# Third attention layer: raw keys stored by token class, loaded without copies in two buffers, spread by a broadcast

## The chip, the cores and the metric

The kernel runs on one core of a Trainium2 chip. The metric is the device time of one execution in microseconds (us); the median of several runs is compared. Engines: PE (TensorE) multiplies matrices, DVE (VectorE), ACT (ScalarE) and POOL (GpSimd) work on tiles of 128 partitions in the on-chip memory, SP (SyncE) issues the DMAs here. SPq and its like in the rows are the queues of an engine, in which DMAs are issued. Each engine executes its own instructions in order and waits on semaphores.

## The reference, cut to what matters

Four pairs of an attention and a feed-forward layer on 2048 tokens of width 128, each with layer norms and a residual. The change lies in the attention layer of the third pair, which sees 4 batches of 512 tokens with 16 heads of width 8:

```python
qkv = (x @ w_qkv.T).reshape(B, N, 3, H, hd).transpose(2, 0, 3, 1, 4)
q, k, v = (qkv[0] * scale, qkv[1], qkv[2])
attn = jnp.einsum('bhid,bhjd->bhij', q, k)
idx = _rp_bucket(N)[None, None]              # clip(j - i, -31, 31) + 31
qL = jnp.einsum('bhid,hdm->bhim', q, rpe_k_table)
attn = attn + jnp.take_along_axis(qL, idx, axis=-1)
kL = jnp.einsum('bhjd,hdm->bhjm', k * scale, rpe_q_table)
attn = attn + jnp.swapaxes(jnp.take_along_axis(kL, idx, axis=-1), 2, 3)
attn = jax.nn.softmax(attn, axis=-1)
out = jnp.einsum('bhij,bhjd->bhid', attn, v)   # + a term of rpe_v_table
```

The term kL belongs to a key j and depends on the distance to the query i. Near the diagonal (distance up to 31) it differs from entry to entry; these are the key bands.

## The kernel before, in words

`l2_attn` is one stage of the program, with a prep block and a main block. P is 128 partitions, T * P is 2048 tokens, B is 4, N is 512, HD is 8, GRP is 32, HALF is 16.

The prep block makes queries, keys and values for all heads, one pass per batch. ACT evacuates PE's products (`L2262` to `L2265`); the fourth of these, `L2265`, writes the scaled keys in float32 into a buffer of two slots, `base[:, b % 2, 2, :]`. PE multiplies it with `gw` (`L2297`), and SP stores it to the DRAM tensor `k32` (`L2157`), 128 rows of 512 tokens. It is the first of ten stores of a batch; the others (`L2160`, `L2164`) write bfloat16 parts of queries and keys. Two semaphores, `stored`, count them by slot; from the third batch on ACT waits for all stores of the batch before last. After them come the stores of `g` and `rv`. The block ends when all engines and stores are done.

The main block runs over 16 heads of 8 steps each, every engine through its own loop over the steps. In a step PE computes the scores of two blocks of 32 queries in all batches (`scores`), DVE adds the band (`L2526`), takes the maximum (`L2528`) and later transposes the probabilities (`L2535`) that ACT has made with exp (`L2609`). Between these PE has other work in its fixed order: in the steps 1 to 3 of head h the key bands of head h+1 (`key_bands`, `L2652`, three rounds), in steps 4 to 7 the query bands of head h+3, and the products with the values.

For the key bands each token's key must stand alone on its partitions. There are 16 classes of tokens, the token number modulo 16. Tile `xk` has on partition 8 i + d component d of the keys, with all tokens zero but those of class 15 - i. It is made per head by three things: SP's `keys(h)` loads `rawk`, in which each of the 8 rows of the head stands 16 times (a source dimension with step 0; 8 KB per partition), and behind it `kshift`, both waited on by semaphores; `expand(h)` on POOL multiplies `rawk` with the mask `own_shift` into `xk` (`L2465`); PE waits for it before the first round. There is one `rawk` and one `xk`. `expand(h + 2)` stands in POOL's order in step 7 of head h, behind `combine(h + 1)` (`L2473`, `L2475`: waits for the load of the query bands `qb` and for the key bands `kb`), `values(h + 1)` (`L2451`, `L2455`) and `cut` (`L2480`: waits for the load of `sb`, the probabilities near the diagonal). `keys(h + 2)` stands in SP's order in step 4 of head h, behind the loads of `qs` and `ks` for head h+1 (`L2350` to `L2354`) and the stores and loads of `pband` (`L2394` to `L2407`). The sources of `qb` and `sb` are skewed: 4 batches, then 32 rows, then the elements.

Of the kernel before, what the change touches and what calls it, by code (L numbers as in the profile page):

```python
# [7 lines left out]
F32 = mybir.dt.float32  # L8
# [6 lines left out]
B = 4  # L15
# [2037 lines left out]
def l2_scratch(nc):  # L2053
    return {"q3": nc.dram_tensor("l2_q3", (P, len(Q_PARTS), T * P), BF16).ap(),
            "k3": nc.dram_tensor("l2_k3", (P, len(K_PARTS), 2, T * P), BF16).ap(),
            "g3": nc.dram_tensor("l2_g3", (2, HEADS, 3, T * P), BF16).ap(),
            "k32": nc.dram_tensor("l2_k32", (P, T * P), F32).ap(),
            "rel": nc.dram_tensor("l2_rel", (P, KEY_SHIFTS), F32).ap(),
            "rv": nc.dram_tensor("l2_rv", (HEADS, P, BAND), F32).ap(),
            "qband": nc.dram_tensor("l2_qband", (QBAND_RING, P, ROW + GRP), F32).ap(),  # L2060
            "pband": nc.dram_tensor("l2_pband", (PBAND_RING, P, HROW + GRP), F32).ap()}


def l2_attn(nc, xs, c, w, scratch):
# [4 lines left out]
    with ExitStack() as ctx:  # L2069
# [18 lines left out]
                 "ones_ready once_ready hl0 hl1 kl kt0 kt1 rl0 rl1 l_ps l_ready qw0 qw1 qw2 qr0 qr1 pw0 pw1 pw2 sr0 sr1 tabq_ready "  # L2088
# [4 lines left out]
        head_loaded = [m["hl0"], m["hl1"]]  # L2093
        shifts_loaded = [m["kt0"], m["kt1"]]
# [16 lines left out]
        with ExitStack() as prep, nc.Block() as block:  # L2111
# [19 lines left out]
            def _(sp):  # L2131
# [22 lines left out]
                for b in range(B):  # L2154
                    cols = slice(b * N, (b + 1) * N)
                    sp.wait_ge(m["base_ready"], 4 * b + 4)
                    sp.dma_start(k32[:, cols], base[:, b % 2, 2, :]).then_inc(stored[b % 2], 16)  # L2157
# [89 lines left out]
            def _(a):  # L2247
# [7 lines left out]
                for b in range(B):  # L2255
# [9 lines left out]
                    a.activation(base[:, b % 2, 2, :], ps_q[1], ACT.Copy, scale=SCALE).then_inc(m["base_ready"], 1)  # L2265
# [10 lines left out]
            def _(pe):  # L2276
# [14 lines left out]
                for b in range(B):  # L2291
# [5 lines left out]
                    pe.matmul(ps_g[2 * HEADS * b:2 * HEADS * (b + 1), :], gw[:, :, :].rearrange("p a h -> p (a h)"), base[:, b % 2, 2, :], start=True, stop=True).then_inc(m["gam_ps"], 1)  # L2297
# [13 lines left out]
        rawk = s.sb("rawk", [P, T * P])  # L2311
# [19 lines left out]
        with nc.Block() as block:  # L2331
            @block.sync
            def _(sp):
                def keys(h):

                    if h:
                        sp.wait_ge(m["xk_ready"], h)
                    src = bass.AP(k32.tensor, k32.offset + h * HD * T * P, [[0, HALF], [T * P, HD], [1, T * P]])
                    sp.dma_start(rawk[:, :], src).then_inc(m["kl"], 16)
# [100 lines left out]
            def _(g):  # L2440
# [19 lines left out]
                def expand(h):  # L2460

                    g.wait_ge(m["kl"], 16 * (h + 1))
                    if h:
                        g.wait_ge(m["l_ps"], ROUND["k", h - 1, KEY_ROUNDS - 1])
                    g.tensor_tensor(xk[:, GRP:GRP + T * P].rearrange("p (g c) -> p g c", c=HALF), rawk[:, :].rearrange("p (g c) -> p g c", c=HALF),  # L2465
# [949 lines left out]
```

## Time and profile before

| | |
|---|---|
| median of 3 runs | 2537.59 us (2532.54 to 2545.24) |
| the profiled execution's own time | 2533.08 us |
| its span, first to last instruction | 2531.3 us |
| mean granted TensorE clock | 0.859 |
| busy: PE, DVE, ACT, POOL | 1916.8, 1696.1, 1089.0, 851.6 us |
| `L2465`, the expansion, 16 times | 72.2 us busy, 73.9 us of waiting for `rawk` before |
| loads of `rawk` | 16 of 1024 KB, 13.3 us from issue to landing in the median |

In all rows times are microseconds from the start of the span. "[3.85 <-POOL l2a_xk L2465]" means that the engine had been idle for 3.85 us, ended by what POOL's line 2465 wrote. PE's records may be slightly off, as matmuls are pipelined. The stage of the change is found in the span from about 1464 to 2050 us.

### The profile page before, as it was taken

Reading aid. Unit: us, or ns where it says so; the run is one execution under the profiler, and the core shown is the slowest. Engines: PE = TensorE matmul, PEld = TensorE weight load, DVE = VectorE, ACT = ScalarE, POOL = GpSimd, SP = SyncE. Lnnn points to the kernel's source line nnn. Section 1 sums busy time; section 2 is a strip of 40 time slices with the busy share of each in tenths; the row PEclk is TensorE's granted clock in tenths of the full one; section 3 lists DMA queues with packets and bytes.
Section 4 is the critical chain, followed back from the end, with each engine's and each line's share of the span. In section 5 each row is a group of like instructions: output and inputs, shape, how many; then the busy total and the mean of one; then the engine's idle time right before and its main releaser. Section 6 shows DMA issues by size and latency. Waiting matters only on the chain. (4 is left out here: it accounts for less than half of the span.)

```text
span 2531.3 us, 46421 instructions
## 1 busy us (share of the span) xinstructions
PE 1916.8 (76%) x16420; PEld 1318.0 (52%) x16420; DVE 1696.1 (67%) x4018; ACT 1089.0 (43%) x2022; POOL 851.6 (34%) x630
## 2 busy tenths in 40 slices
PE   5888886587778876449999846878878747999666
PEld 2555554255555553337777614444444336888444
DVE  4777777676555564668999951788887857223574
ACT  2666664354445542204444421555555412333442
POOL 3000000774455430113344333445454319900211
PEclk8999999799999898659999965698888757999678
DMA  3011110200000000010000046566665432000000
GB/s 104 30 39 40 40 38 2 80 16 16 16 16 16 16 16 1 5 22 11 21 21 16 5 133 172 145 175 174 169 178 166 119 122 89 26 8 1 6 1 19
DMA packets 126969, 144.92 MB, mean 57 GB/s; under 512 B 73222, under 2 KB 100673, under 8 KB 123992
## 3 DMA queue, kind: packets, MB, share of 16 engines
q1 hardware_dynamic: 123542, 132.82, 18.9%
q10 hardware_dynamic: 3266, 9.96, 1.0%
q8 instruction: 99, 1.62, 0.3%
q14 instruction: 62, 0.51, 0.1%
HBM read 94.46 MB, written 40.81 MB: 53 GB/s over the span
## 5 line engine op out<-in xcount | busy, mean ns | idle before, releaser
L454 ACT ACTIVATE l0a_pr<-l0a_sm,l0a_nm 128x512 f32<-128x512 f32 x256 | 185.1, 724 | 142.6 <-DVE l0a_nm L367 142.1
L367 DVE CUSTOM_DVE_ANT_0 l0a_sm<-l0a_ps_s,l0a_tb 128x512 f32<-128x512 f32 x256 | 170.8, 685 | 87.6 <-PE l0a_ps_s L522 84.7
L2609 ACT ACTIVATE l2a_pr<-l2a_ps_s,l2a_nm 128x512 f32<-128x512 f32 x256 | 173.8, 685 | 116.6 <-DVE l2a_nm L2528 115.6
L530 PE MATMUL l0a_ps_p<-top_c_ident,l0a_pr 128*128 128x128 f32 x1024 | 168.9, 288 | 54.4 <-ACT l0a_pT L462 54.2
L530 PEld LDWEIGHTS l0a_ps_p<-top_c_ident,l0a_pr 128*128 128x128 f32 x1024 | 109.3, 142 | 116.5 <-ACT l0a_pr L454 65.1
L2528 DVE TENSOR_REDUCE l2a_nm<-l2a_ps_s 128x2 f32<-128x1024 f32 x128 | 156.7, 1224 | 4.4
L2535 DVE STREAM_TRANSPOSE l2a_tt<-l2a_pr 128x1024 f32<-128x1024 f32 x128 | 158.0, 1234 | 0.1
L1557 POOL TENSOR_TENSOR l1f_h<-l1f_lm,l1f_sg 128x512 f32<-128x512 f32 x72 | 92.5, 1285 | 184.9 <-DVE l1f_lm L1626 184.9
L807 POOL TENSOR_TENSOR l0f_ct<-l0f_raw,l0f_cos_scaled 128x1024 f32<-128x1024 f32 x32 | 76.7, 2397 | 174.0 <-issue 94.2
L1929 ACT ACTIVATE l2f_h<-l2f_ps_h 128x512 f32<-128x512 f32 x128 | 76.5, 598 | 135.8 <-PE l2f_ps_h L1474 129.8
L1684 ACT ACTIVATE l1f_csb<-l1f_ps_c,l1f_b3e 128x512 f32<-128x512 f32 x128 | 88.1, 688 | 106.0 <-PE l1f_ps_c L1474 105.7
L2705 PE MATMUL l2a_ps_o<-l2a_tt,l2a_vd 128*32 128x256 f32 (+7 forms) x1472 | 124.3, 376 | 0.0
L1042 PE MATMUL l0f_ps_side<-l0f_wqkv,l0f_hT 128*128 128x512 f32 x192 | 110.5, 667 | 15.9 <-ACT l0f_hT L953 9.5
L2526 DVE TENSOR_TENSOR l2a_ps_s<-l2a_ps_s,l2a_qb 128x192 f32<-128x192 f32 (+2 forms) x160 | 45.7, 304 | 113.2 <-PE l2a_ps_s L2676 69.0
L1887 DVE SCALAR_TENSOR_TENSOR l2f_acc<-l2f_ps_y,l2f_comb,l2f_acc 128x128 f32<-128x128 f32 x112 | 31.5, 344 | 134.0 <-PE l2f_ps_y L1967 134.0
L1967 PEld LDWEIGHTS l2f_ps_y<-l2f_w2T,l2f_h 128*128 128x128 f32 x1024 | 119.1, 192 | 2.8
L1967 PE MATMUL l2f_ps_y<-l2f_w2T,l2f_h 128*128 128x128 f32 x1024 | 119.3, 275 | 0.0
L336 POOL COPY l0a_vh<-l0a_va 128x128 f32 x14 | 4.1, 293 | 326.6 <-PE l0a_ps_o L541 326.6
L2652 PE MATMUL l2a_ps_l<-l2a_xk,l2a_kshift 128*32 128x256 f32 x768 | 74.0, 519 | 50.5 <-POOL l2a_xk L2465 48.2
L522 PE MATMUL l0a_ps_s<-l0a_ks,l0a_qs 48*128 48x512 bf16 x256 | 100.9, 395 | 8.1 <-issue 7.6
L823 POOL TENSOR_TENSOR l0f_rn<-l0f_ss,top_c_half 128x16 f32<-128x16 f32 x32 | 95.0, 2970 | 33.5 <-DVE l0f_ss L904 32.5
L2465 POOL TENSOR_TENSOR l2a_xk<-l2a_rawk,l2a_masks 128x2048 f32<-128x2048 f32 x16 | 72.2, 4515 | 73.9 <-DMA l2a_rawk<-l_k 73.9
(522 smaller groups left out, 5190.5 us busy)
## 6 DMA issues: line engine op xcount, KB each, us to landing
l2a_rawk<-l_k SPq DMA_DIRECT2D x16, 1024.0 KB, 13.3
l2a_qb<-l_qband SPq DMA_DIRECT2D x16, 768.0 KB
l2a_sb<-l_pband SPq DMA_DIRECT2D x32, 384.0 KB
l_qband<-l2a_staged SPq DMA_DIRECT2D x14, 768.0 KB, 15.1
l0a_tb<-l_bias SPq DMA_DIRECT2D x16, 448.0 KB
l2a_ks<-l_k SPq DMA_DIRECT2D x16, 384.0 KB
l_pband<-l2a_pr SPq DMA_DIRECT2D x32, 192.0 KB, 8.7
l_pband<-l2a_pr SPq DMA_DIRECT2D x32, 144.0 KB, 2.2
```

The lines of the kernel that those rows point to most:

```text
L367: v.tensor_tensor_reduce(sm[j % 4][:, :], ps_s[j % 2][:, :], tb[slot][:, off:off + N][:, ::-1], -1.0, 3e38, ALU.add, ALU.min, nm[:, j % 4: ...
L454: a.activation(pr[j % 4][:, :], sm[j % 4][:, :], ACT.Exp, bias=nm[:, j % 4:j % 4 + 1], scale=-1.0).then_inc(m["p_ready"], 1)
L522: pe.matmul(ps_s[j % 2][:, :], qs[slot][:, b * N + it * P:b * N + (it + 1) * P], ks[slot][:, b * N:(b + 1) * N], start=True, stop=True).th ...
L530: last = pe.transpose(ps_p[j % 2][:, tile(k)], pr[j % 4][:, tile(k)], ident[:, :])
L823: g.tensor_tensor(rn[:, u, :], ss[:, u, :], c["half"][:, :], ALU.pow).then_inc(m["rn_ready"], 1)
L1042: last = pe.matmul(bank[:, :], hT[:, tile(t)], wqkv[:, l, i * F_INNER:(i + 1) * F_INNER], start=True, stop=True)
L1557: g.tensor_tensor(h[b % 2][:, k, :], lm[:, k, :], sg[:, k, :], ALU.mult).then_inc(h_ready, 1)
L1967: last = pe.matmul(ps_y[b % 2][:, t, :], h[b % 2][:, k, t * P:(t + 1) * P], w2T[slot][:, k, :], start=(k == 0), stop=(k == FC - 1))
L2528: v.tensor_reduce(nm[:, g % 2, :], ps_s[g % 2][:, :, :], AX, ALU.max, negate=True).then_inc(m["nm_ready"], 1)
L2535: v.transpose(tt[n % 2][:, u * NB:(u + 2) * NB, :].rearrange("p (u k) i -> p u (k i)", u=2), pr[g // 2 % PR_RING][:, 2 * (g % 2):2 * (g % ...
L2609: a.activation(pr[slot][:, 2 * (g % 2) + u, :], ps_s[g % 2][:, u, :], ACT.Exp, bias=nm[:, g % 2, u:u + 1], accum_out=rs[:, n % 2, 2 * (g % ...
L2705: last = pe.matmul(ps_o[n % 2][GRP * g:GRP * (g + 1), (lo - a0) * GRP:(hi - a0) * GRP], vd[h % 2][:, v, k, :], tt[n % 2][:, block:block + ...
```

## The change

The raw keys are stored, loaded and read in another layout.

- Store: `L2265` writes the keys of a batch sorted by class, class 15 first, and SP stores them to `k32`, now (128, 16 classes, 4 batches, 32 tokens): runs of 32 elements, 128 bytes. PE's product with `gw` reads the sorted keys through a view that gives the tokens in their old order and writes to the same places.
- Load: partition 8 i + d gets only the tokens of class 15 - i, 128 elements, 512 bytes, without copies. There are two `rawk` buffers with a semaphore each, and the wait ahead of the load is for the expansion two heads earlier.
- Expansion: POOL's first operand is the loaded 128 elements, each read 16 times in a row by a broadcast; mask, output and count of elements stay.

```diff
--- before.py
+++ after.py
@@ -2054,7 +2054,7 @@
     return {"q3": nc.dram_tensor("l2_q3", (P, len(Q_PARTS), T * P), BF16).ap(),
             "k3": nc.dram_tensor("l2_k3", (P, len(K_PARTS), 2, T * P), BF16).ap(),
             "g3": nc.dram_tensor("l2_g3", (2, HEADS, 3, T * P), BF16).ap(),
-            "k32": nc.dram_tensor("l2_k32", (P, T * P), F32).ap(),
+            "k32": nc.dram_tensor("l2_k32", (P, HALF, B, N // HALF), F32).ap(),
             "rel": nc.dram_tensor("l2_rel", (P, KEY_SHIFTS), F32).ap(),
             "rv": nc.dram_tensor("l2_rv", (HEADS, P, BAND), F32).ap(),
             "qband": nc.dram_tensor("l2_qband", (QBAND_RING, P, ROW + GRP), F32).ap(),
@@ -2085,12 +2085,13 @@
         ps_l = s.ps("ps_l", [P, N])
         names = ("w_loaded t_loaded m_loaded rv_loaded zero_ready zeroed wt_ready wT_ready zb_ready t_ready zT_ready qk_ps base_ready hi_ready res_ready "
                  "mid_ready lo_ready q_lo gam_ps gam_ready g_lo g_stored v_ps va_ready tab_ready tab_stored rvd_ready rvd_stored st0 st1 "
-                 "ones_ready once_ready hl0 hl1 kl kt0 kt1 rl0 rl1 l_ps l_ready qw0 qw1 qw2 qr0 qr1 pw0 pw1 pw2 sr0 sr1 tabq_ready "
+                 "ones_ready once_ready hl0 hl1 kl0 kl1 kt0 kt1 rl0 rl1 l_ps l_ready qw0 qw1 qw2 qr0 qr1 pw0 pw1 pw2 sr0 sr1 tabq_ready "
                  "s_ps biased nm_ready p_ready tT xk_ready added comb_ready sm_ready vs_ready masked st_ready vd_ready pv_done o_ps oe_ready u_ps rr_ready o_done "
                  "at_ps aoT_ready y_ps y_ready dve")
         m = {n: s.sem(n) for n in names.split()}
         ident = c["ident"]
         head_loaded = [m["hl0"], m["hl1"]]
+        keys_loaded = [m["kl0"], m["kl1"]]
         shifts_loaded = [m["kt0"], m["kt1"]]
         rv_slot_loaded = [m["rl0"], m["rl1"]]
         qband_read = [m["qr0"], m["qr1"]]
@@ -2154,7 +2155,7 @@
                 for b in range(B):
                     cols = slice(b * N, (b + 1) * N)
                     sp.wait_ge(m["base_ready"], 4 * b + 4)
-                    sp.dma_start(k32[:, cols], base[:, b % 2, 2, :]).then_inc(stored[b % 2], 16)
+                    sp.dma_start(k32[:, :, b, :], base[:, b % 2, 2, :].rearrange("p (c g) -> p c g", c=HALF)).then_inc(stored[b % 2], 16)
                     sp.wait_ge(m["q_lo"], b + 1)
                     for first, count, part in Q_ROW_RUNS:
                         sp.dma_start(q3[:, first:first + count, cols], parts[:, b % 2, 0, part:part + 1, :].broadcast_to([P, count, N])).then_inc(stored[b % 2], 16)
@@ -2262,7 +2263,8 @@
                     a.activation(q32[:, :, b, :], by_block(ps_q[0]), ACT.Copy, scale=SCALE).then_inc(m["base_ready"], 1)
                     a.activation(base[:, b % 2, 0, :], ps_q[1], ACT.Identity, bias=rel[:, 0, last:last + 1]).then_inc(m["base_ready"], 1)
                     a.activation(base[:, b % 2, 1, :], ps_q[1], ACT.Identity, bias=rel[:, 0, 0:1]).then_inc(m["base_ready"], 1)
-                    a.activation(base[:, b % 2, 2, :], ps_q[1], ACT.Copy, scale=SCALE).then_inc(m["base_ready"], 1)
+                    a.activation(base[:, b % 2, 2, :].rearrange("p (c g) -> p g c", c=HALF)[:, :, ::-1], ps_q[1].rearrange("p (g c) -> p g c", c=HALF),
+                                 ACT.Copy, scale=SCALE).then_inc(m["base_ready"], 1)
                     for i in range(3):
                         a.wait_ge(m["base_ready"], 4 * b + i + 1)
                         if i == 0:
@@ -2294,7 +2296,8 @@
                     for i in range(2):
                         pe.matmul(ps_q[i].rearrange("p (k j) -> p k j", j=GRP), wT[:, i, :], zT[:, :, b, :], start=True, stop=True).then_inc(m["qk_ps"], 1)
                     pe.wait_ge(m["base_ready"], 4 * b + 4)
-                    pe.matmul(ps_g[2 * HEADS * b:2 * HEADS * (b + 1), :], gw[:, :, :].rearrange("p a h -> p (a h)"), base[:, b % 2, 2, :], start=True, stop=True).then_inc(m["gam_ps"], 1)
+                    pe.matmul(ps_g[2 * HEADS * b:2 * HEADS * (b + 1), :].rearrange("p (g c) -> p g c", c=HALF), gw[:, :, :].rearrange("p a h -> p (a h)"),
+                              base[:, b % 2, 2, :].rearrange("p (c g) -> p g c", c=HALF)[:, :, ::-1], start=True, stop=True).then_inc(m["gam_ps"], 1)
                 for i in range(NB // 4):
                     if i:
                         pe.wait_ge(m["va_ready"], i)
@@ -2308,7 +2311,7 @@
         ones3 = s.sb("ones3", [3, T * P], BF16)
         qs = s.sb("qs", [2 * (P // 2), T * P], BF16)
         ks = s.sb("ks", [2 * (P // 2), 2, T * P], BF16)
-        rawk = s.sb("rawk", [P, T * P])
+        rawk = [s.sb(f"rawk{i}", [P, T * P // HALF]) for i in range(2)]
         xk = s.sb("xk", [P, GRP + T * P + GRP + HALF])
         kshift = [s.sb(f"kshift{i}", [P, WINDOW_COLS]) for i in range(2)]
         staged = [s.sb(f"staged{i}", [P, NB, BAND]) for i in range(2)]
@@ -2333,10 +2336,11 @@
             def _(sp):
                 def keys(h):
 
-                    if h:
-                        sp.wait_ge(m["xk_ready"], h)
-                    src = bass.AP(k32.tensor, k32.offset + h * HD * T * P, [[0, HALF], [T * P, HD], [1, T * P]])
-                    sp.dma_start(rawk[:, :], src).then_inc(m["kl"], 16)
+                    if h >= 2:
+                        sp.wait_ge(m["xk_ready"], h - 1)
+                    each = T * P // HALF
+                    src = bass.AP(k32.tensor, k32.offset + h * HD * T * P, [[each, HALF], [T * P, HD], [1, each]])
+                    sp.dma_start(rawk[h % 2][:, :], src).then_inc(keys_loaded[h % 2], 16)
                     if h >= 2:
                         sp.wait_ge(m["l_ps"], ROUND["k", h - 2, KEY_ROUNDS - 1])
                     src = bass.AP(rel_d.tensor, rel_d.offset + h * HD * KEY_SHIFTS, [[1, HALF], [KEY_SHIFTS, HD], [1, WINDOW_COLS]])
@@ -2459,10 +2463,10 @@
 
                 def expand(h):
 
-                    g.wait_ge(m["kl"], 16 * (h + 1))
+                    g.wait_ge(keys_loaded[h % 2], 16 * (h // 2 + 1))
                     if h:
                         g.wait_ge(m["l_ps"], ROUND["k", h - 1, KEY_ROUNDS - 1])
-                    g.tensor_tensor(xk[:, GRP:GRP + T * P].rearrange("p (g c) -> p g c", c=HALF), rawk[:, :].rearrange("p (g c) -> p g c", c=HALF),
+                    g.tensor_tensor(xk[:, GRP:GRP + T * P].rearrange("p (g c) -> p g c", c=HALF), rawk[h % 2][:, :].unsqueeze(2).broadcast_to([P, T * P // HALF, HALF]),
                                     own_shift.unsqueeze(1).broadcast_to([P, T * P // HALF, HALF]), ALU.mult).then_inc(m["xk_ready"], 1)
 
                 def combine(h):
```

## Rows read from the trace of the kernel before

**Rows 1.** The page: its first line.

```profile
span 2531.3 us, 46421 instructions
```

**Rows 2.** Busy time by engine in a window: stretch, its length, then PE, PEld, DVE, ACT, POOL, clock, DMA share, GB/s.

```profile
1636.21:1979.68 343.47, 275.06 (x3954) 160.70 (x3952) 285.22 (x385) 181.19 (x488) 165.53 (x120) 0.87 0.62 172
```

**Rows 3.** The timeline, DVE, one step of head 2: start, length, engine, line, operation.

```profile
1652.05 0.35 DVE L2526 TENSOR_TENSOR l2a_ps_s<-l2a_ps_s,l2a_qb 128x192 f32<-128x192 f32 x1
...
1654.74 0.33 DVE L2526 TENSOR_TENSOR l2a_ps_s<-l2a_ps_s,l2a_qb 128x192 f32<-128x192 f32 x1
```

**Rows 4.** The list of waits, 1450 to 2150 us: who, for whom, us in total, times, longest.

```profile
POOL l2a_xk L2465 <- DMA l2a_rawk<-l_k: 73.9, 15, 8.7
...
DVE l2a_ps_s L2526 <- PE l2a_ps_s L2676: 69.0, 42, 4.4
...
PE l2a_ps_l L2652 <- POOL l2a_xk L2465: 48.2, 14, 7.8
```

**Rows 5.** The timeline of heads 2 and 3, SP, POOL, PE and DVE.

```profile
1651.71 0.56 SPq L2339 DMA_DIRECT2D l2a_rawk<-l_k  x1
...
1660.12 0.73 POOL L2480 TENSOR_TENSOR l2a_sb<-l2a_sb,l2a_masks 128x256 f32<-128x256 f32 x1 [2.38 <-DMA l2a_sb<-l_pband]
...
1661.92 0.21 PE L2671 MATMUL l2a_ps_s<-l2a_ks,l2a_qs 51*32 51x32 bf16 x4 [0.71 <-DMA l2a_ks<-l_g]
...
1665.05 4.52 POOL L2465 TENSOR_TENSOR l2a_xk<-l2a_rawk,l2a_masks 128x2048 f32<-128x2048 f32 x1 [4.20 <-DMA l2a_rawk<-l_k]
...
1669.71 1.72 PE L2652 MATMUL l2a_ps_l<-l2a_xk,l2a_kshift 128*32 128x256 f32 x16 [3.85 <-POOL l2a_xk L2465]
...
1672.48 0.37 DVE L2526 TENSOR_TENSOR l2a_ps_s<-l2a_ps_s,l2a_qb 128x192 f32<-128x192 f32 x1 [3.04 <-PE l2a_ps_s L2676]
```

**Rows 6.** The timeline, DVE: first and second waits of four heads.

```profile
1643.85 0.36 DVE L2526 TENSOR_TENSOR l2a_ps_s<-l2a_ps_s,l2a_qb 128x192 f32<-128x192 f32 x1 [3.18 <-PE l2a_ps_s L2676]
...
1648.15 0.36 DVE L2526 TENSOR_TENSOR l2a_ps_s<-l2a_ps_s,l2a_qb 128x192 f32<-128x192 f32 x1 [1.53 <-PE l2a_ps_s L2676]
...
1676.13 0.37 DVE L2526 TENSOR_TENSOR l2a_ps_s<-l2a_ps_s,l2a_qb 128x192 f32<-128x192 f32 x1 [0.87 <-PE l2a_ps_s L2676]
...
1871.47 0.37 DVE L2526 TENSOR_TENSOR l2a_ps_s<-l2a_ps_s,l2a_qb 128x192 f32<-128x192 f32 x1 [0.26 <-PE l2a_ps_s L2676]
...
1876.41 0.37 DVE L2526 TENSOR_TENSOR l2a_ps_s<-l2a_ps_s,l2a_qb 128x192 f32<-128x192 f32 x1 [2.02 <-PE l2a_ps_s L2676]
...
1987.33 0.37 DVE L2526 TENSOR_TENSOR l2a_ps_s<-l2a_ps_s,l2a_qb 128x192 f32<-128x192 f32 x1 [3.25 <-PE l2a_ps_s L2676]
...
1992.21 0.37 DVE L2526 TENSOR_TENSOR l2a_ps_s<-l2a_ps_s,l2a_qb 128x192 f32<-128x192 f32 x1 [2.11 <-PE l2a_ps_s L2676]
```

**Rows 7.** The DMA issues: count, KB each, median us from issue to landing.

```profile
l2a_rawk<-l_k SPq DMA_DIRECT2D x16, 1024.0 KB, 13.3
...
l2a_kshift<-l_rel SPq DMA_DIRECT2D x16, 56.0 KB, 12.9
```

**Rows 8.** Busy time in a window of one microsecond, columns as in rows 2.

```profile
1748.00:1749.00 1.00, 0.32 (x8) 0.00 (x0) 1.00 (x2) 0.59 (x2) 0.00 (x0) 1.00 0.23 95
```

**Rows 9.** The groups by line, POOL: count, busy us, mean ns, idle before.

```profile
L2455 POOL TENSOR_TENSOR l2a_vd<-l2a_vs,l2a_masks 128x512 f32<-128x512 f32 x32 | 32.6, 1039 | 1.3
```

**Rows 10.** Windows of the prep block: zeros written, stores of a batch, the last store.

```profile
1494.00:1495.00 1.00, 1.00 (x2) 0.46 (x2) 0.96 (x3) 0.00 (x0) 0.92 (x2) 0.50 0.22 33
...
1505.00:1512.00 7.00, 4.31 (x5) 1.35 (x6) 3.79 (x5) 3.78 (x7) 2.38 (x3) 0.50 1.03 343
...
1532.00:1533.00 1.00, 1.00 (x7) 0.99 (x5) 0.00 (x0) 0.00 (x0) 0.00 (x0) 0.50 1.02 262
```

**Rows 11.** The timeline of the prep block: ACT's third pass, DVE's last copy.

```profile
1505.40 0.60 ACT L2262 ACTIVATE l2a_q<-l2a_ps_s 128x512 f32<-128x512 f32 x1 [12.22 <-issue]
...
1536.19 0.69 DVE L2242 COPY l2a_va<-l2a_ps_s 128x512 f32<-128x512 f32 x1 [2.17 <-PE l2a_ps_s L2302]
```

**Rows 12.** The groups by line, PE, in the prep block.

```profile
L2297 PE MATMUL l2a_ps_l<-l2p_base,l2p_gw 128*32 128x512 f32 x8 | 6.1, 854 | 18.4 <-ACT l2p_base L2265 18.4
```

## The prediction

> **What bounds the kernel now.** The program is a row of stages, and all that is changed lies in one of them, the third attention layer. So I left the page's totals after one look at the span [rows 1] and asked for one long stretch of that stage: twelve heads, from one head's key expansion to the same instruction twelve heads later [rows 2]. It lasts 343.47 us, 28.62 us a head, and VectorE is busy for 285.22 us of it, 23.77 us a head. No other engine comes near once PE's time is read with care: PE shows 275.06 us busy, but its clock was granted at 0.87.
>
> VectorE's own floor follows from its instructions [rows 3]. A step (add the band, find the maximum, transpose) runs from 1652.05 to 1654.74 when nothing is late, 2.69 us. A head has 8 such steps, 21.5 us; band transposes and normalisations are the rest of the 23.8 us. The other 4.8 us of a head are waits, and the list of waits names them [rows 4]: VectorE waited 69.0 us, in 42 waits, for PE's scores; PE waited 48.2 us, 14 times, for the expanded keys of GpSimd (`xk`); and GpSimd waited 73.9 us, 15 times, for the load of the raw keys (`rawk`).
>
> One head shows that this is one chain [rows 5]. The load is issued at 1651.71. GpSimd has nothing else to do from the end of its mask multiply (1660.12 + 0.73 = 1660.85), idles 4.20 us for the load, and expands from 1665.05 to 1669.57. PE, in order, stands for 3.85 us before the key bands, and the next scores are queued behind them; VectorE gets those 3.04 us late. Over heads 2 to 14 that VectorE wait occurs 13 times, from 3.18 us in the first to 3.25 us in the last, least 0.26, and sums to 33.4 us [rows 6]. Each is followed one or two steps later by a second, from 1.53 us in the first head to 2.11 in the last, least 0.87, 21.3 us in 13 waits [rows 6]: PE is behind by a key round, a third of a value product and a by-token step. Head 0 has 3.1 us, and 11.2 us are spread over the rest.
>
> **The change part by part.**
> *The load (13 of the 15 waits, from head 2 on).* 1024 KB with 16 copies of each row become 64 KB in 512-byte pieces. The issue stands at the same place of SP's order, so it is not earlier; only the landing is. The old one took 13.3 us in the median. The small load issued just behind it, `kshift`, 56 KB, took 12.9 us [rows 7]: most of both is queueing, not bytes. So the new one costs between "nothing in the queue" (lands before 1660.85, GpSimd's free moment) and kshift's 12.9 us (1664.6, a gain of 0.4 us only). What can be worked out of the relief: in the quietest microseconds the DMA engines show 0.23 of 16 busy at 95 GB/s [rows 8], some four engines at 24 GB/s each that are at work even then. A sixteenth of the old load, 64 KB on each, is 2.7 us at that rate. The new load then lands 13.3 - 2.7 = 10.6 us after its issue at the latest, at 1662.3, and the backlog that it meets is itself shorter by as much of the last head's. I take 1661. Expansion then ends at 1665.0 to 1665.5, while PE came to its wait at 1669.71 - 3.85 = 1665.86: the wait is gone in this head.
> But what remains of the head gets shorter too. If the second wait (1.5 us) and PE's 0.71 us for `ks` [rows 5] go as well, PE is there at 1663.6 and waits up to 1.7 us. I take 0.6 us a head as left. Gain of the first wait: 33.4 - 13 x 0.6 = 25.6 us; ends 13 x 0.4 = 6 (kshift's landing) and 33.4.
> The Trainium skill ("DMA: Bandwidth & Descriptors", section "Why a DMA increments its semaphore by 16 and not by 1") says that a DMA uses as many engines, up to 16, as divide the slowest dimension of both its patterns. By it the skewed `qb` and `sb` loads, whose slowest dimension is the 4 batches, sit on four engines, which agrees with the 0.23 in the trace, and the new load (slowest dimension 16) has a share on those four and must stand behind them: it would be the rival "queue" below.
>
> *The second wait.* PE's clock falls after its long waits: over the twelve heads the granted clock is 0.87 [rows 2], so part of every head runs at the lower of its two levels (1.2 instead of 2.4 GHz), and the round behind the wait of 3.85 us took 1.72 us for 16 matmuls [rows 5]; the smallest second waits (0.87) stand against 1.64 in the mean (21.3 / 13). If half the heads reach 0.9 I gain 13 x 0.4 = 5 us; ends 0 and 21.
> *The rest of the 69.0.* Keys and queries of the next head come sooner with less in the queue; 2 us, ends 0 and 11.
> *The multiply itself.* Its first operand becomes a broadcast along the innermost dimension. The value multiply (L2455) has such operands and takes 1039 ns for 512 elements, 2.03 ns each [rows 9]; the present one 4.52 us for 2048, 2.21 each. So 4.2 us, bounds 4.2 to 4.5; it counts once, in head 0, where the expansion follows the first combine and PE's wait of up to 7.8 us is not for a load: 0.4 us.
> *Two buffers.* In SP's order `keys(1)` no longer waits for the first expansion; what stands behind it waits for ACT's evacuations anyway. 0 us, bounds 0 and 1.
>
> *The price in the prep block.* The four stores of `k32` become 2048 pieces of 128 bytes each instead of 128 of 2 KB. This block is bound by its stores: the DMA engines stand at 1.03 and 343 GB/s [rows 10], and ACT's third pass at 1505.40 waits 12.22 us for the first batch's stores [rows 11]. The old store is 262 KB at 343 GB/s, 0.8 us. For 128-byte pieces the nearest row is the writing of zeros to DRAM: share 0.22 at 33 GB/s, so 258 pieces in a microsecond for 3.5 engines, 13.6 ns each; 2048 of them on 16 engines take 1.75 us, 0.95 more. The dear end is the 384-byte store at 1.02 and 262 GB/s, 682 pieces in a microsecond, 24 ns: 3.06 us, 2.3 more. One or two such stores stand before the later passes, four before the block's end; its last copy starts at 1536.19 [rows 11], 3.2 us after the last microsecond in which the DMA engines are full [rows 10]. Loss: 1 us at the least, 4 x 2.3 = 9 at the most; I take 2, two cheap stores ahead of the later passes.
> The Trainium skill (same page, "Specifications") asks for 512 bytes and more, as smaller writes are read, changed and written back. That speaks against this store; if each piece is handled like 512 bytes, a store is, as an estimate from that page, 1 MB at 343 GB/s, 3.1 us, and the forecast up to 7 us longer. The zeros at 13.6 ns don't show such a price, but they ran on a queue that was nearly empty.
> ACT writes the same 512 elements strided and PE reads them so in four matmul pairs. ACT's neighbour L2262 writes in runs of 32 at 0.60 us, no more than the others [rows 11]; PE's eight records are 6.1 us in all [rows 12]. I take 0; twice the time in both would be 6.1 + 4 x 0.6 = 8.5 us, of which the two batches on the path carry half, 4.
>
> **Sum.** 25.6 + 5 + 2 + 0.4 - 2 = 31 us. The profiled run has 2533.1 us around its 2531.3 us span, 4.5 under the median of 2537.6; taken from the median: 2506.6, and I say 2506.
>
> **The rivals.**
> 1. *Everything unwinds.* PE waits no more, its clock stays up, the second waits fall to nearly nothing: head = 23.8 + 0.6. 33.4 + 18 + 8 - 2 = 57 us: 2481. For it: the first wait can be as short as 0.26 us. Against it: in that same head the second one is still 2.02 us [rows 6].
> 2. *The queue takes the place of the copies.* The small load still stands behind `sb`, `qs` and `ks` on the busy engines, or GpSimd's mask multiply before the expansion, which itself waited for `sb` until 1660.12, becomes late in the shorter head. Then 1.7 us of each head stay: 33.4 - 22 + 4 - 2 = 13 us: 2524.
> 3. *The change doesn't do what it says:* the broadcast read is dear on GpSimd. At 4.5 us more the expansion ends where it did. Against it stands L2455. No gain, prep loss 2: 2540.
> 4. *Slower.* The scattered stores in the saturated prep queue cost more than the loop gains. The gain of 33 us is used up at 8.3 us more a store, 9.1 us for 128 pieces on each engine, 71 ns a piece, five times the zeros and three times the 384-byte row. At 100 ns: 12.8 - 0.8 = 12 us each, 48 - 33 = 15 slower: 2552.
>
> **How the numbers follow.** Forecast 0.55 (own range 2492 to 2516), rival 1 0.17, rival 2 0.17, rival 3 0.06, rival 4 0.05. The range runs from 2480 (rival 1) to 2528, behind rival 2 and half of the prep's dear end. What a measurement of this kernel can tell from no change is about 0.5%, 12.7 us: faster is under 2525. Forecast, rival 1 and over half of rival 2 lie there: 0.82; within: 0.13; slower: 0.05.
>
> **What would show it.** Right: GpSimd's wait for `rawk` under 10 us in all, PE's for `xk` under 15, head period near 26.4 us in the same kind of stretch, VectorE's wait for scores at 35 to 40 us, the expansion at 4.2 us, four `k32` stores that make the prep block 2 us longer. Wrong: a landing of `rawk` over 11 us (rival 2), an expansion over 5 us (rival 3), a prep block longer by over 9 us (rival 4). What would make the forecast wrong altogether is that VectorE's second wait grows by what the first one loses.

## The result, and the profile after

The changed kernel takes 2501.3 us in the median (2500.0 to 2507.5) against 2535.1 us for the kernel before: ratio 0.987, 95% interval 0.9849 to 0.989. That is 33.8 us less. The forecast was 2506 us, with a range of 2480 to 2528, so the number held. As the waits and the experiments show, the path to it held only in part.

The first line of the changed kernel's page, then the window of twelve heads, from one expansion (1634.15) to the one twelve heads on (1948.82), columns as in [rows 2]:

```profile
span 2505.5 us, 46421 instructions
```

```profile
1634.15:1948.82 314.67, 259.88 (x3952) 155.40 (x3948) 285.84 (x384) 181.12 (x488) 155.03 (x120) 0.91 0.49 151
```

Twelve heads take 314.67 us where they took 343.47 [rows 2]: 26.22 us a head instead of 28.62. VectorE is as busy as before, 285.84 us against 285.22, so its 23.8 us a head are now 91% of the time. The granted clock rose from 0.87 to 0.91.

The list of waits of the changed kernel (who, for whom, us in total, times, longest):

```profile
POOL l2a_qb L2477 <- DMA l2a_qb<-l_qband: 163.9, 16, 26.5
...
POOL l2a_sb L2484 <- DMA l2a_sb<-l_pband: 59.3, 19, 6.8
...
PE l2a_ps_s L2675 <- DMA l2a_ks<-l_g: 36.1, 14, 4.0
...
DVE l2a_st L2545 <- POOL l2a_sb L2484: 20.0, 13, 5.0
...
DVE l2a_ps_s L2530 <- PE l2a_ps_s L2680: 19.3, 24, 2.2
...
POOL l2a_xk L2469 <- DMA l2a_rawk<-l_k: 18.4, 14, 3.7
...
PE l2a_ps_l L2656 <- POOL l2a_xk L2469: 14.4, 8, 7.1
```

Four lines of the same list for the kernel before, which [rows 4] does not show:

```profile
POOL l2a_qb L2473 <- DMA l2a_qb<-l_qband: 114.7, 12, 20.5
...
POOL l2a_sb L2480 <- DMA l2a_sb<-l_pband: 33.4, 15, 7.1
...
PE l2a_ps_s L2671 <- DMA l2a_ks<-l_g: 13.2, 12, 3.0
...
DVE l2a_st L2541 <- POOL l2a_sb L2480: 5.9, 3, 4.5
```

Three lines of the changed kernel answer to [rows 4]. GpSimd's wait for `rawk` fell from 73.9 to 18.4 us, PE's for `xk` from 48.2 to 14.4 (half of it in head 0), VectorE's for the scores from 69.0 to 19.3. The others grew: GpSimd waits 163.9 us for `qb`, which was 114.7, and 59.3 us for `sb`, which was 33.4; PE waits 36.1 us for the next head's `ks`, which was 13.2; and VectorE waits 20.0 us for GpSimd's masked `sb`, which was 5.9. VectorE's two waits, for the scores and for the masked `sb`, fell together from 74.9 to 39.3 us. That is nearly the whole gain of the loop: from VectorE's first step to its last band transpose it went from 462.52 us (1580.96 to 2043.48) to 426.05 (1585.73 to 2011.78), 36.5 us less.

Landings (median us from issue), the store of the keys, the expansion, ACT's and PE's strided instructions (minimum, median and maximum in ns):

```profile
l2a_rawk<-l_k SPq DMA_DIRECT2D x16, 64.0 KB, 9.6
...
l2a_kshift<-l_rel SPq DMA_DIRECT2D x16, 56.0 KB, 9.2
...
l_k<-l2p_base SPq DMA_DIRECT2D x4, 256.0 KB, 4.1
...
L2469 POOL TENSOR_TENSOR l2a_xk<-l2a_rawk,l2a_masks x16: 3664/3672/3674, 1547.9 to 1948.8; 128x2048 f32<-128x2048 f32 x16
...
L2266 ACT ACTIVATE l2p_base<-l2a_ps_s x4: 1037/1038/1039, 1484.8 to 1519.1; 128x512 f32<-128x512 f32 x4
...
L2299 PE MATMUL l2a_ps_l<-l2p_base,l2p_gw x8: 1027/1039/1060, 1485.9 to 1521.1; 128*32 128x512 f32 x8
```

The load lands after 9.6 us, where 13.3 stood in [rows 7]; 64 KB alone can't need that, and `kshift` of 56 KB behind it takes 9.2. The expansion takes 3.67 us for 2048 elements, not 4.52 as in [rows 5]: 1.79 ns each. ACT's fourth evacuation takes 1.04 us, 0.607 before; PE's products with it have a median of 1.04 us, 0.88 before.

The prep block runs from VectorE's first statistics to its last copy:

```profile
1466.31 0.87 DVE L140 BATCH_NORM_STATS2 l2a_ln_stats<-top_xs 128x6 f32<-128x128 f32 x4 [1.16 <-PEq L53]
...
1540.79 0.69 DVE L2243 COPY l2a_va<-l2a_ps_s 128x512 f32<-128x512 f32 x1 [2.17 <-PE l2a_ps_s L2305]
```

1540.79 - 1466.31 = 74.5 us. In the kernel before it was 1536.19 - 1464.74 = 71.5 us [rows 11], so the block grew by 3.0 us.

The two profiled executions differ by 25.8 us in their spans, less than the medians, because the profiled execution of the changed kernel (2507.5 us) is the slowest of its four. Where it lost that can be seen. It came to the stage 1.6 us late, and it lost 6.4 us in the next feed-forward layer, between the third and the fourth issue of the weight load `w1n` there (SP, L1836). They lie at 2046.70 and 2102.76, 56.1 us apart; in the kernel before they lie at 2079.50 and 2129.14, 49.6 us apart. The profiles of `e1_one_buffer`, `e3_plain_operand`, `e4_bytes_besides` and `e5_bytes_distinct`, all from one chip, show 55.0 to 56.2 us here, those of the other eight runs, from another chip, 49.1 to 51.5. No experiment was made on this, and its cause stays open; it lies outside the loop and the prep block, from which the gain is read.

### The profile page after: what moved, and what is told of

Its sections match the earlier page's. It is cut to its first block and busy times, and to the rows that moved or that the text cites. A ratio compares the mean times of both kernels' runs of the same rounds, so it can differ in the third digit from the quotient of the medians.

```text
span 2505.5 us, 46421 instructions
## 1 busy us (share of the span) xinstructions
PE 1891.1 (75%) x16420; PEld 1304.2 (52%) x16420; DVE 1698.2 (68%) x4018; ACT 1090.4 (44%) x2022; POOL 836.8 (33%) x630
## 5 line engine op out<-in xcount | busy, mean ns | idle before, releaser
L2709 PE MATMUL l2a_ps_o<-l2a_tt,l2a_vd 128*32 128x256 f32 (+7 forms) x1472 | 116.0, 357 | 0.0
L375 DVE COPY l0a_pT<-l0a_ps_p 128x512 f32<-128x512 f32 x128 | 87.8, 686 | 4.3 <-issue 3.5
L2643 PE MATMUL l2a_ps_l<-l2a_tabq,l2a_q 128*128 128x96 f32 x512 | 83.1, 312 | 7.7 <-ACT l2a_pr L2592 3.4
## 6 DMA issues: line engine op xcount, KB each, us to landing
l2f_upw<-in_L_ffn_up_weights ACTq DMA_DIRECT2D x9, 512.0 KB, 12.4
```

The lines of the kernel that those rows point to most:

```text
L2709: last = pe.matmul(ps_o[n % 2][GRP * g:GRP * (g + 1), (lo - a0) * GRP:(hi - a0) * GRP], vd[h % 2][:, v, k, :], tt[n % 2][:, block:block + ...
```

## The experiments

The theory of the prediction was a chain: the load's landing, the expansion, PE's wait, VectorE's wait. The profile after suggested another one, called Q here: some few DMA engines, which carry the skewed loads of `qb` and `sb`, are full, and everything that is queued with them comes late, whatever waits for it. The experiments set these against each other, and each part of the change against the rest.

**e1_one_buffer: the changed kernel with one `rawk` buffer.**

The edit, shortened (the expansion waits for and reads the one buffer likewise):

```diff
-                    if h >= 2:
-                        sp.wait_ge(m["xk_ready"], h - 1)
+                    if h:
+                        sp.wait_ge(m["xk_ready"], h)
 ...
-                    sp.dma_start(rawk[h % 2][:, :], src).then_inc(keys_loaded[h % 2], 16)
+                    sp.dma_start(rawk[0][:, :], src).then_inc(keys_loaded[0], 16)
```

> The changed kernel with one rawk buffer in place of two (the load of head h waits for the expansion of head h-1, as before). Theory (the gain is the small load's): in SP's order the load stands in step 4 and the wait has long been met, so nothing changes: 2501 us, within 3. Rival (the second buffer matters): the load is issued later or holds up the stores behind it in SP's queue, 2505 to 2515.

Measured: 2504.6 us (2494.1 to 2508.1), ratio 0.9876 (0.9849 to 0.9904), which is the changed kernel's. The second buffer is worth nothing that can be measured.

**e2_before_two_buffers: the kernel before with two buffers for its old load.** The edit is the reverse of the one above, on the kernel before, with both tiles of 2048 elements.

> The kernel before with two buffers for the old load of 1024 KB, and no other part of the change. Theory (the load's place in SP's order and its 13 us in the queues set the landing, not the buffer): no change, 2532 to 2537. Rival (the buffer carries part of the gain): 2505 to 2525.

Measured: 2533.4 us, ratio 0.9986 (0.9972 to 1.0): no difference. Its list of waits is that of [rows 4]:

```profile
POOL l2a_xk L2466 <- DMA l2a_rawk<-l_k: 74.0, 15, 8.6
...
PE l2a_ps_l L2653 <- POOL l2a_xk L2466: 46.7, 14, 7.7
```

The buffer is out, in both directions.

**e3_plain_operand: the changed kernel, with the expansion's first operand from a plain tile.** The plain tile `full` holds ones, so this kernel leaves out the key bands' dependence on the keys; load, waits and all else stay. The edit, shortened:

```diff
-                    g.tensor_tensor(xk[...], rawk[h % 2][:, :].unsqueeze(2).broadcast_to([P, T * P // HALF, HALF]),
+                    g.tensor_tensor(xk[...], full[:, :].rearrange("p (g c) -> p g c", c=HALF),
```

> The changed kernel, but the expansion reads its first operand from a plain tile of 2048 ones instead of the broadcast of the loaded keys; load, waits and all else stay (the key bands are then computed from ones, so that part of the computation is left out). The operation should go back from 3.67 to 4.51 us. Rival A (the faster multiply carries part of the gain, 0.84 us a head on the way to PE): 16 x 0.84 = 13 us slower, 2514. Theory (GpSimd's end has some slack, PE waits for xk only 14.4 us in 8 waits): 2 to 8 us slower, 2503 to 2509. Nothing at all, 2501, if the loop is bound elsewhere.

Measured: 2507.4 us, ratio 0.9902 (0.9886 to 0.9919). The expansion's durations, and PE's wait for it:

```profile
L2472 POOL TENSOR_TENSOR l2a_xk<-l2a_full,l2a_masks x16: 4502/4528/4541, 1546.3 to 1947.6; 128x2048 f32<-128x2048 f32 x16
...
PE l2a_ps_l L2659 <- POOL l2a_xk L2472: 22.0, 11, 7.8
```

The operation went back to 4.53 us and PE's wait for `xk` from 14.4 to 22.0 us. But the loop did not get longer by it. Two more waits of this kernel:

```profile
DVE l2a_ps_s L2533 <- PE l2a_ps_s L2683: 31.7, 31, 3.1
...
DVE l2a_st L2548 <- POOL l2a_sb L2487: 9.9, 6, 5.4
```

VectorE waits 12.4 us more for the scores and 10.1 us less for the masked `sb`, and its loop takes 427.4 us (1583.73 to 2011.13), against 426.1 in the changed kernel and 427.1 in `e1_one_buffer` (1584.90 to 2012.01). In whole times it is 2.8 us above `e1_one_buffer` on the same chip, and the two intervals overlap. So the faster multiply is worth nothing that these runs can tell; 13 us, the first expectation, do not fit the loops, and between the middle one and "nothing at all" the runs do not decide.

**e4_bytes_besides: the changed kernel, and the old megabyte besides, for nobody.** The megabyte goes into a tile `spare` that no engine reads. The edit, shortened:

```diff
                     sp.dma_start(kshift[h % 2][:, :], src).then_inc(shifts_loaded[h % 2], 16)
+                    if h:
+                        sp.wait_ge(m["sp_done"], 16 * h)
+                    src = bass.AP(k32.tensor, k32.offset + h * HD * T * P, [[0, HALF], [T * P, HD], [1, T * P]])
+                    sp.dma_start(spare[:, :], src).then_inc(m["sp_done"], 16)
```

> The changed kernel, and behind kshift also the old load of 1024 KB with its 16 copies of each row, into a tile that nobody reads or waits for. Theory Q (the megabyte cost its time in the DMA queues, on the few engines that also carry the skewed loads of qb and sb): most of the gain is lost although no engine waits for these bytes, 2515 to 2535, with longer landings of sb, ks and rawk. Theory W (only the landing of rawk itself counted, as the first wait of the prediction's sum): 2501 to 2508.

Measured: 2537.0 us, ratio 1.0015 (1.0002 to 1.0028). The whole gain is gone, and the time is 2 us above the range that theory Q was given, though no compute engine waits for these bytes, and the keys are loaded small, ahead of them. Its window of twelve heads and three of its waits:

```profile
1631.90:1978.55 346.65, 266.96 (x3952) 157.83 (x3946) 286.64 (x384) 181.18 (x488) 155.48 (x121) 0.85 0.62 173
...
PE l2a_ps_s L2681 <- DMA l2a_ks<-l_g: 68.5, 13, 6.8
...
DVE l2a_st L2551 <- POOL l2a_sb L2490: 43.0, 16, 4.8
...
PE l2a_ps_l L2662 <- POOL l2a_xk L2475: 10.5, 7, 7.3
```

A head is at 346.65 / 12 = 28.89 us. PE hardly waits for `xk` (10.5 us); it waits 68.5 us for `ks`, and VectorE 43.0 us for the masked `sb`. So PE's 48.2 us for `xk` in the kernel before were one place where the queue's lateness came out, and not its cause: remove that wait and keep the bytes, and the same time is spent at other waits. Theory W, which the prediction's first term stands on, falls. Of Q this run shows one half, that the bytes cost time in the queue whoever waits for them; that it is a matter of few engines is left to `e7_split_after` and `e8_split_before`.

**e5_bytes_distinct: as `e4_bytes_besides`, the megabyte read from 128 different rows.**

```diff
-                    src = bass.AP(k32.tensor, k32.offset + h * HD * T * P, [[0, HALF], [T * P, HD], [1, T * P]])
+                    src = bass.AP(k32.tensor, k32.offset, [[T * P, P], [1, T * P]])
```

> As e4_bytes_besides, but the megabyte is read from 128 different rows instead of 16 times from the same 8. Same bytes, same pieces of 8 KB, same 16 engines. If only bytes and pieces count, the time is that of e4_bytes_besides within 3 us. If reading one row 16 times was what made the old load dear, this one is nearer to 2501, by 5 us or more under e4_bytes_besides.

Measured: 2517.6 us, ratio 0.9932 (0.9914 to 0.995), 19.4 us under `e4_bytes_besides` on the same chip. Window and wait:

```profile
1633.30:1966.47 333.17, 263.76 (x3952) 157.43 (x3952) 287.03 (x387) 181.42 (x488) 155.34 (x120) 0.89 0.61 180
...
PE l2a_ps_s L2681 <- DMA l2a_ks<-l_g: 54.5, 13, 5.5
```

27.76 us a head. Same bytes, same piece size, same number of pieces; the only difference is whether a row is read once or 16 times. Against `e1_one_buffer` (2504.6 us), which has no megabyte and ran on the same chip, the megabyte costs 32 us. Of these 13 (2517.6 - 2504.6) are the bytes, the pieces and the issue of one more DMA a head, and 19 are the repeated reading of the same 64 KB.

**e6_store_2k: the changed kernel with `k32` stored in pieces of 2 KB, and gathered by the load in runs of 128 bytes.** The edit, shortened (the store and the tile's side of the load follow the layout):

```diff
-            "k32": nc.dram_tensor("l2_k32", (P, HALF, B, N // HALF), F32).ap(),
+            "k32": nc.dram_tensor("l2_k32", (P, B, HALF, N // HALF), F32).ap(),
 ...
-                    each = T * P // HALF
+                    each = N // HALF
-                    src = bass.AP(k32.tensor, k32.offset + h * HD * T * P, [[each, HALF], [T * P, HD], [1, each]])
+                    src = bass.AP(k32.tensor, k32.offset + h * HD * T * P, [[each, HALF], [T * P, HD], [N, B], [1, each]])
```

> The changed kernel with k32 laid out (128, 4 batches, 16 classes, 32 tokens), so that a batch is stored in 128 pieces of 2 KB as before, and the load gathers 4 pieces of 128 bytes for each partition (512 pieces a head in place of 128 of 512 bytes). Theory (128-byte writes cost the prep block its extra 3 us, reads of 128 bytes into the chip are cheap): the prep block's last copy comes 2 to 3 us sooner, 2498 to 2501. Rival (the price of the prep block is ACT's strided write of 1.04 us and PE's strided read, not the stores): no change in the prep block, and 512 pieces a load make the loop 0 to 5 us longer, 2501 to 2507.

Measured: 2499.3 us (2488.2 to 2502.7), ratio 0.9841 (0.9817 to 0.9865). Its prep block:

```profile
1468.33 0.87 DVE L140 BATCH_NORM_STATS2 l2a_ln_stats<-top_xs 128x6 f32<-128x128 f32 x4 [1.16 <-PEq L53]
...
1540.33 0.69 DVE L2243 COPY l2a_va<-l2a_ps_s 128x512 f32<-128x512 f32 x1 [2.17 <-PE l2a_ps_s L2305]
```

1540.33 - 1468.33 = 72.0 us, against 74.5 with the 128-byte stores and 71.5 before. The stores cost the block 2.5 us, ACT's and PE's strided accesses 0.5 us, as the theory had it. The other profiles agree: 74.4 to 74.7 us wherever the stores are in pieces of 128 bytes, 72.0 in `e9_split_store`. On the whole kernel 2 us can't be told from none.

**e7_split_after and e8_split_before: each skewed load as four DMAs, one for each batch.** The same edit on the changed kernel and on the kernel before; `sb` likewise; the waits count 4 times as much. The edit for `qb`, shortened:

```diff
-                    src = skewed(qband[h % QBAND_RING], GRP - 1, -1, ROW)
-                    sp.dma_start(qb[h % 2][:, :, :].rearrange("p a n -> p (a n)"), src).then_inc(qband_read[h % 2], 16)
+                    for b in range(B):
+                        src = skewed_batch(qband[h % QBAND_RING], GRP - 1, -1, ROW, b)   # [[pitch + step, GRP], [1, width]]
+                        sp.dma_start(qb[h % 2][GRP * b:GRP * (b + 1), :, :].rearrange("p a n -> p (a n)"), src).then_inc(qband_read[h % 2], 16)
```

> The changed kernel with each skewed load of qb and sb issued as four DMAs, one for each batch, with 32 rows as the slowest dimension instead of 4 batches. Theory F (the four engines on which the skewed loads sit bound the loop now; PE waits 36 us for ks and DVE 20 us for sb): these waits go, 2470 to 2490. Rival (VectorE's floor of 23.8 us a head and PE's order hold the loop at 26.2): 2497 to 2501. Rival 2 (SP has 9 more issues a head of 0.5 us and becomes late): 2505 or more.

> The kernel before with the same split of qb and sb into four DMAs each, and nothing of the change. Theory F: the old load's wait came from queueing on those four engines; with them free the megabyte lands in 4 to 7 us, GpSimd's wait for it goes and with it most of the 33 us: 2490 to 2505. Rival (the megabyte itself, with its 16 reads of each row, is the cost wherever it runs): 2525 to 2535.

Measured: `e7_split_after` 2464.2 us, ratio 0.9719 (0.9703 to 0.9736), 6 us below the lower end of what theory F gave it; `e8_split_before` 2462.0 us, ratio 0.971 (0.9694 to 0.9726). The profile of `e8_split_before`, which has nothing of the change: twelve heads, two waits, two landings, SP's issues of the `qs` load in ns:

```profile
1619.91:1905.88 285.97, 241.15 (x3937) 150.18 (x3938) 281.05 (x384) 179.94 (x488) 164.98 (x120) 0.98 0.84 206
...
POOL l2a_xk L2472 <- DMA l2a_rawk<-l_k: 57.7, 15, 8.7
...
PE l2a_ps_l L2659 <- POOL l2a_xk L2472: 7.5, 8, 2.7
...
l2a_rawk<-l_k SPq DMA_DIRECT2D x16, 1024.0 KB, 9.4
...
l2a_qb<-l_qband SPq DMA_DIRECT2D x64, 192.0 KB, 3.9
...
L2350 SPq DMA_DIRECT2D l2a_qs<-l_q x16: 419/420/1530, 1557.4 to 1919.7; - x16
```

285.97 / 12 = 23.83 us a head, the floor of VectorE that was worked out from [rows 3]. VectorE is busy for 281.05 of 285.97 us. The old load is still there with its megabyte and its copies and lands after 9.4 us; GpSimd still waits 57.7 us for it. But PE now waits 7.5 us for `xk`: GpSimd's wait is idle time that costs nothing here. `qb` lands after 3.9 us. The expectation of 2490 to 2505 for this kernel was too cautious by 28 us: I had thought that freeing the engines would save what the change saves, and it saves the rest too.

**e10_split_qb and e11_split_sb: one of the two splits alone, on the changed kernel.**

> The changed kernel with only the load of qb (768 KB a head) split by batch. Theory F (the sum of the work on the four engines counts): qb and sb are 768 KB each a head, so this one gives about half or, once the four engines are no longer full, nearly all of the 37 us of the full split: 2465 to 2483. Rival (one particular landing, that of sb, is what the loop waits for): 2495 to 2501.

> The changed kernel with only the loads of sb (2 x 384 KB a head) split by batch. Theory F: 2465 to 2483, like the split of qb alone. Rival (the waits for ks and for qb come from qb's own long load, and sb is only a victim of it): 2495 to 2501.

Measured: `e10_split_qb` 2469.5 us, ratio 0.9736 (0.9721 to 0.9752); `e11_split_sb` 2491.2 us, ratio 0.9819 (0.9795 to 0.9843). The first is where theory F had it. The second fell between its two expectations: both missed. Window and waits of each, `e10_split_qb` first:

```profile
1625.54:1912.85 287.31, 244.60 (x3938) 150.42 (x3936) 281.47 (x384) 178.82 (x488) 155.49 (x120) 0.97 0.62 165
...
POOL l2a_sb L2490 <- DMA l2a_sb<-l_pband: 54.2, 18, 7.3
...
DVE l2a_st L2551 <- POOL l2a_sb L2490: 5.7, 2, 4.9
```

```profile
1633.52:1938.74 305.22, 254.25 (x3952) 154.36 (x3952) 283.30 (x384) 179.42 (x485) 154.11 (x121) 0.93 0.58 155
...
POOL l2a_qb L2483 <- DMA l2a_qb<-l_qband: 199.7, 15, 26.4
...
POOL l2a_sb L2490 <- DMA l2a_sb<-l_pband: 6.1, 1, 6.1
...
DVE l2a_st L2551 <- POOL l2a_sb L2490: 18.4, 9, 2.9
```

Both loads are 768 KB a head, but the split of `qb` brings 32 us and a head of 23.94, that of `sb` 10 us and 25.44. Bytes on the few engines are not all of it. One head of the changed kernel shows what is special with `qb`; SP, GpSimd, PE, VectorE, GpSimd:

```profile
1694.41 5.89 SPq L2354 DMA_DIRECT2D l2a_qs<-l_q  x1
...
1700.35 0.50 SPq L2355 DMA_DIRECT2D l2a_ks<-l_k  x1
...
1702.81 1.28 POOL L2477 TENSOR_TENSOR l2a_qb<-l2a_qb,l2a_masks 128x512 f32<-128x512 f32 x1 [8.97 <-DMA l2a_qb<-l_qband]
...
1710.56 0.72 POOL L2484 TENSOR_TENSOR l2a_sb<-l2a_sb,l2a_masks 128x256 f32<-128x256 f32 x1
...
1710.85 0.21 PE L2675 MATMUL l2a_ps_s<-l2a_ks,l2a_qs 51*32 51x32 bf16 x4 [3.17 <-DMA l2a_ks<-l_g]
...
1711.32 0.98 DVE L2545 STREAM_TRANSPOSE l2a_st<-l2a_sb 128x768 f32<-128x768 f32 x1 [2.00 <-POOL l2a_sb L2484]
...
1711.72 3.67 POOL L2469 TENSOR_TENSOR l2a_xk<-l2a_rawk,l2a_masks 128x2048 f32<-128x2048 f32 x1 [0.44 <-DMA l2a_rawk<-l_k]
```

GpSimd stands for 8.97 us before `combine`, because `qb` lands only then; all its later work of the head is late by that, and when it comes to the mask of `sb` at 1710.56 it needn't wait for `sb` at all, but VectorE has been waiting 2.00 us for it. So part of the 20.0 us for `sb` is `qb`'s. And SP, in the issue of `qs` at 1694.41, is held for 5.89 us, so the load of `ks` behind it is issued at 1700.35 and PE waits for it 3.17 us. With `sb` split alone VectorE still waits 18.4 us for the masked `sb`, though GpSimd waits only 6.1 us for its load; with `qb` split alone it is 5.7 us, though GpSimd waits 54.2. That agrees with the reading. In `e11_split_sb` GpSimd's wait for `qb` even grew, to 199.7 us, while PE waits only 3.9 us for `ks` and SP's issue of `qs` takes 0.42 us in the median: this part of the gain came with the split of `sb` alone.

**e9_split_store and e12_split_before_again: is the change worth anything beside the split?** `e9_split_store` is the changed kernel with the split and the 2 KB stores; `e12_split_before_again` is `e8_split_before`, unchanged.

> The changed kernel with both mends: the skewed loads of qb and sb split by batch, and k32 stored in pieces of 2 KB (the load gathers runs of 128 bytes). The split brings the head to VectorE's floor (24.0 us); the 2 KB store can only give back what the 128-byte pieces cost in the prep block. If that is 0 to 3 us: 2460 to 2464, the same as the split kernel of before (2462) within what can be measured. If the small load is worth something on its own once the four engines are free: 2450 to 2458.

> e8_split_before again, unchanged, on the chip of e9_split_store and with more rounds, to compare the two: 2462, within 3. It tells whether the change is worth anything beside the split: e9_split_store lower by over 4 us if so, equal if the change only relieved engines that the split frees anyway.

Measured: `e9_split_store` 2462.2 us, ratio 0.9705 (0.9691 to 0.9719); `e12_split_before_again` 2458.9 us, ratio 0.9692 (0.9673 to 0.9712). The intervals overlap. With the skewed loads spread, the change has nothing left to give. In the profiles VectorE's loop is even 3 us shorter without it, 391.0 and 391.6 us (`e8_split_before`, `e12_split_before_again`) against 394.4 and 394.8 (`e7_split_after`, `e9_split_store`); why was not tried. The version to keep is the kernel before with the split and nothing else, 77 us or 3.1% under the kernel before.

## Why the prediction was right or wrong, point by point

- **What bounds the kernel.** VectorE's floor of 23.8 us a head was right, and `e8_split_before` reaches it. "This is one chain" was wrong as a cause. The chain from the load to VectorE is what the waits show, but `e4_bytes_besides` keeps the small load, cuts the wait for `xk` to 10.5 us and is as slow as the kernel before.
- **The load.** I took it to land 9.3 us after its issue and it lands after 9.6. Queueing and not bytes was the right reading of `kshift`'s 12.9 us. For the relief I took 2.7 us for each head, worked out as bytes at the quiet rate of [rows 8]. The runs show that the megabyte costs 32 us in 16 loads, 2.0 us each, in the kernel's time (`e4_bytes_besides`); that its greater part, 19 us, is the reading of the same rows 16 times was in no step.
- **First wait, 25.6 us.** VectorE's waits can be sorted by what PE does next: the first wait of a head is for the scores just ahead of PE's second key round, the second for those just ahead of the third. Sorted so, the first waits of heads 2 to 14 fell from 33.4 to 2.0 us (0.97 and 0.99, none in the other heads), 31.4 instead of 25.6. I had left 0.6 us in each head.
- **Second wait, 5 us.** The second waits fell from 21.3 to 5.2 us, 16.1 instead of 5: this term of the sum was the one most under its size. The clock rose from 0.87 to 0.91, and with the skewed loads split it is at 0.98 (`e8_split_before`).
- **The rest, keys and queries of the next head sooner, +2 us.** VectorE's other waits for scores outside head 0 fell from 11.2 to 9.9 us, so the size is near, but the reason was wrong in sign: the keys came later, and PE's wait for `ks` grew by 22.9 us. Their load stands behind SP's issue of `qs`, which is held.
- **The term that was missing.** VectorE's waits for the scores fell by 49.7 us in all, where 33 were forecast. Against that, 14.1 us came back as its wait for the masked `sb`, a wait that I had at nothing outside of rival 2.
- **The multiply, 4.2 us.** It was 3.67. In head 0, where I counted it, the wait for scores fell by 0.9 us (3.08 to 2.23) against 0.4 forecast; `e3_plain_operand` finds nothing more in the loop that can be told from the scatter.
- **Two buffers, 0 us.** Right (`e1_one_buffer`, `e2_before_two_buffers`).
- **The prep block, -2 us.** It is 3.0 us: 2.5 for the stores, 0.5 for the strided accesses, which I had taken as 0. ACT's neighbour L2262, with runs of 32 elements, was the wrong row for writes whose neighbours lie 128 bytes apart: 1.04 us and not 0.60. The cheap price, 0.95 us a store, was the nearer one: the landing grew by 1.3 us, from 2.8 to 4.1. The Trainium skill ("DMA: Bandwidth & Descriptors", "Specifications") says that below 512 bytes the DMA engines read, change and write back. The estimate of 2.3 us a store that I drew from it was too high, against 1.3 in the landing and 2.5 us for all four stores in the block; whether the pieces are read first no run shows.
- **The sum.** 31 us forecast, 33.8 measured. In the loop 33 were forecast and 36.5 came, as 49.7 less 14.1, and 0.9 at other places; the block took 3.0 where I had 2. The waits for scores unwound nearly as far as rival 1 has them, and a wait outside of the sum took a part back. These two errors have opposite signs and nearly met, so the number was met in good part by luck.
- **The signs.** Right: PE's wait for `xk` under 15 us (14.4), a head near 26.4 us (26.22), a landing under 11 us (9.6). The prep block was to grow by 2 us and grew by 3.0. Missed: GpSimd's wait for `rawk` under 10 us (18.4), VectorE's wait for scores at 35 to 40 us (19.3), the expansion at 4.2 us (3.67).
- **Rival 2, the queue takes the place of the copies**, had the right mechanism in its second half, GpSimd's mask multiply that comes late, with the wrong size: priced at 22 us, it took back 14 (masked `sb`) from a larger gain. The skewed loads on few engines, which I named in its support, are what holds the changed kernel, as `e7_split_after` shows with 37 us: [rows 8] showed 0.23 of 16 engines at 95 GB/s in the quietest microseconds, and I used that line as a rate when it was the finding.
- **Rivals 3 and 4** did not come: the broadcast read is faster, and a 128-byte piece costs nowhere near 71 ns.

## What to carry to other kernels

When loads queue behind a few busy DMA engines, a wait that is long in the profile may be only where the lateness comes out. Before a load is made smaller, ask which engines carry the loads beside it: a DMA whose slowest dimension is 4 kept to few engines here (a share of 0.23 to 0.25 of 16), and its issue as four DMAs with 32 rows each brought 75 us here where a sixteenfold smaller load brought 34 and then nothing more. A microsecond in which the DMA share is 0.23 to 0.25 again and again was the sign here. An unused transfer put beside the kernel is a cheap test of whether bytes or a wait count.

## What the runs showed of the hardware that I had not expected

SP's issue of a DMA can be held. The issue of the `qs` load takes these times in the changed kernel, minimum, median and maximum in ns, and below it stands one microsecond inside the held issue of 1694.41:

```profile
L2354 SPq DMA_DIRECT2D l2a_qs<-l_q x16: 504/5813/6788, 1563.1 to 1958.5; - x16
...
1696.00:1697.00 1.00, 1.00 (x22) 0.53 (x19) 1.00 (x2) 0.93 (x4) 0.00 (x0) 1.00 0.25 92
```

The median is 5.8 us; it was 1.5 in the kernel before and is 0.42 us in `e8_split_before`. It is no wait for a semaphore: the one ahead of the load of head 5 asks for the scores up to head 3, and SP's store at 1692.94, ahead of the held issue at 1694.41, already needed probabilities of head 4. The issue is held where the skewed loads ahead of it are under way at a share of 0.25, and all later DMAs of SP's queue stand behind it, although three quarters of the DMA engines are idle. It takes both skewed loads: with `qb` alone or `sb` alone split the median is 0.46 and 0.42 us. What inside the issue waits, no run shows. The changed kernel holds it longer than the kernel before, whose first waits gave the queue time to drain; that last clause is a reading of the two profiles and wasn't tried by itself.

Reading the same 8 rows of DRAM 16 times costs more than reading 128 different rows once: 19.4 us in 16 loads, 1.2 us for each megabyte, with bytes and pieces the same (`e4_bytes_besides`, `e5_bytes_distinct`).

GpSimd's multiply with a first operand that stays the same for 16 elements takes 1.79 ns an element, with a plain operand 2.21 ns (3.67 us in the changed kernel and 4.52 in the kernel before, for 2048).
